# Attention and expert layer on one core: the maxima are transposed in the value bank, and the latents' softmax is normalised behind its product with the values

## What is computed

```python
local  = softmax over the last 128 keys (q k / 4) @ v          # 16 heads
pooled = mean of every 16 tokens                               # 64 latents a batch
lscores = rq rk / 4, only latents of earlier chunks allowed    # 4 heads of 16
lattn  = softmax(lscores);  lattn = 0 where no latent is allowed
remote = (lattn @ rv) @ rout_w + rout_b
gate   = sigmoid(local @ gl_w + remote @ gr_w)
mixed  = gate * local + (1 - gate) * remote
x1     = x + ga * (mixed @ out_w + out_b)
```

## Time and profile before

| what | value |
|---|---|
| median of the runs shown | 576.77 us (572.23 to 577.25, 3 runs) |
| the profiled execution's own time | 576.64 us |
| its span, first to last instruction | 574.9 us |
| busy: PE, DVE, ACT, POOL | 84%, 76%, 62%, 66% of the span |
| mean granted TensorE clock | 0.949 of full speed |

### The profile page before, as it was taken

How to read it: one execution, slowest core, us unless ns; L and a number is a source line. 1 busy time by engine, 2 the same in 40 slices (tenths; PEclk the granted TensorE clock), 3 DMA queues, 4 the chain that set the end, 5 groups by cost and what they waited for, 6 DMA issues and landing times.

```text
span 574.9 us, 19855 instructions
## 1 busy us (share of the span) xinstructions
PE 482.9 (84%) x7168; PEld 364.1 (63%) x7168; DVE 436.6 (76%) x1193; ACT 353.8 (62%) x868; POOL 379.2 (66%) x516
## 2 busy tenths in 40 slices
PE   2446689999899999999999999999999999988771
PEld 2205567777677666777777676777776676766451
DVE  2155657788688888988988788888888887878554
ACT  1210466677677667777777577777776776766540
POOL 2222346778577767788877587777777677766663
PEclk9975889999899999999999899999999999999776
DMA  9558644618244444434252607162534444440000
GB/s 277 114 133 246 163 105 99 132 47 187 56 113 75 95 94 93 94 90 93 64 101 68 119 34 145 39 125 62 120 68 97 92 94 93 82 79 10 11 10 19
DMA packets 56523, 55.15 MB, mean 96 GB/s; under 512 B 7380, under 2 KB 53100, under 8 KB 54892
## 3 DMA queue, kind: packets, MB, share of 16 engines
q1 hardware_dynamic: 53564, 52.57, 41.4%
q10 hardware_dynamic: 2864, 1.31, 1.1%
HBM read 37.07 MB, written 16.80 MB: 94 GB/s over the span
## 4 chain that ended last, share of the span: by engine, by line
PE 72%; issue 11%; POOL 5%; DVE 4%; DMA 2%; ACT 2%; ACTq 1%; SPq 1%; POOLq 0%; DVEq 0%
PE p_pv L819 9%; PE p_qkv L730 9%; PE p_qkv L740 6%; PE p_misc L886 6%; PE p_y L806 5%; PE p_x L785 5%; PE p_y L807 5%; PE p_x L778 4%; PE p_a L751 3%; PE p_qkv L860 3%; PE p_misc L869 2%; PE p_a L831 2%; PE p_a L716 2%; PE p_misc L877 2%; PE p_a L753 2%
## 5 line engine op out<-in xcount | busy, mean ns | idle before, releaser
L592 ACT ACTIVATE pr<-p_y 128x512 f32<-128x512 f32 x224 | 124.6, 595 | 55.8 <-PE p_y L807 52.9
L1159 DVE TENSOR_REDUCE mtok<-p_x 128x3 bf16<-128x480 f32 (+1 forms) x192 | 109.3, 585 | 30.9 <-PE p_x L785 29.6
L441 POOL TENSOR_SCALAR_AFFINE_SELECT pr<-pr 128x512 f32<-128x512 f32 x128 | 89.6, 701 | 11.2 <-ACT pr L594 9.0
L451 POOL TENSOR_TENSOR rstd<-ve,half 128x1 f32<-128x1 f32 x96 | 58.1, 605 | 47.9 <-DVE ve L1079 47.7
L469 POOL TENSOR_TENSOR dif<-local,rem 128x272 f32<-128x272 f32 x32 | 30.9, 965 | 83.8 <-DVE local L1197 83.8
L445 POOL TENSOR_SCALAR_AFFINE_SELECT pr<-pr 128x512 f32<-128x512 f32 x112 | 81.3, 726 | 0.0
L807 PE MATMUL p_y<-qst,kst 112*128 112x128 bf16 x512 | 73.2, 221 | 0.0
L806 PE MATMUL p_y<-qst,kst 112*128 112x128 bf16 x448 | 66.5, 221 | 7.7 <-ACT pr L592 4.8
L819 PE MATMUL p_pv<-pr,vp 128*18 128x128 f32 x1920 | 67.1, 279 | 2.1 <-POOL pr L445 0.8
L730 PE MATMUL p_qkv<-hT,wqk 128*128 128x256 f32 x256 | 66.1, 403 | 2.2 <-DVE qkf L1111 1.3
L740 PE MATMUL p_qkv<-wv,hT 128*128 128x272 f32 x128 | 40.1, 439 | 29.5 <-issue 29.4
(11 more groups left out here) (131 smaller groups left out, 1092.7 us busy)
## 6 DMA issues: line engine op xcount, KB each, us to landing
scr_q<-terms SPq DMA_DIRECT2D x16, 384.0 KB, 2.5
qst<-scr_q SPq DMA_DIRECT2D x16, 384.0 KB, 4.7
scr_k<-terms SPq DMA_DIRECT2D x16, 384.0 KB, 4.4
kst<-scr_k SPq DMA_DIRECT2D x16, 384.0 KB, 5.4
qst<-scr_q SPq DMA_DIRECT2D x16, 256.0 KB, 5.4
kst<-scr_k SPq DMA_DIRECT2D x16, 256.0 KB, 6.4
out_y<-y SPq DMA_DIRECT2D x32, 128.0 KB, 1.7
x_all<-in_x SPq DMA_DIRECT2D x3, 1024.0 KB, 8.3
```

The costliest lines, as they stand in the source:

```text
L441: ins = pool.affine_select(out=own, in_=own, compare_op=ALU.is_ge, fill=0.0, base=-1, pattern=[[0, 4], [1, P]], channel_multiplier=-1)
L592: act.activation(pr[:, 2 * i:2 * i + 2, :, :], src, ACT.Exp).then_inc(exp_done[i], 1)
L1159: dve.tensor_reduce(mtok[:, KS + h0:KS + h1], p_x[i % 2][:, 0:(h1 - h0) * w].rearrange("p (h n) -> p h n", n=w), AX_X, ALU.max, negate=Tru ...
```

## The change

- `max_t` writes to `p_pv` instead of `p_qkv`, and stands behind part 1 of the scores instead of ahead of it. It waits for `oT_ready` of the tile before (`out_t` has emptied the bank). `mtok` has two buffers now. `shift` reads `p_pv`; ScalarE's list keeps its order but for what is removed.
- `project_v` waits for `rem_ready` of k-3 instead of `shift`; `lat_remote` waits for `shift` no more.
- The latents' softmax is not divided before its product with the values. `lat_exp` sums no rows, `lat_p_t` transposes the exponentials `le` themselves, and `bvd` has 64 more columns of ones by head, so that `lat_out_t` puts the sums of each head into rows 64 to 127 of `p_misc`. `lat_recip` is now the reciprocal of these 64 x 128 values, `lat_norm` the product with it, and both work on tile `m` on VectorE between `norm1` and `maxima` part 3. The product writes `loT`; ScalarE's `lat_oT` is gone. In the first tile of a batch 16 columns are set to zero by an instruction of their own.
- In the setup four copies put the ones into the two buffers of `bvd` and of a new `bvd1` (for tiles that see 32 latents).

```diff
@@ ScalarE
-                act.activation(q_of(t)[KS:KS + H, :, :], p_qkv[KS:KS + H, 0:P // 2]...
+                act.activation(q_of(t)[KS:KS + H, :, :], p_pv[KS:KS + H, 0:P // 2]...
...
-                act.wait_ge(lp_ready, done(t - 1))
+                act.wait_ge(lpT_psum, done(t - 1))
                 for h in range(LH):
-                    ins = act.activation(..., ACT.Exp, bias=lneg[:, h:h + 1], accum_out=lsum[:, h:h + 1])
+                    ins = act.activation(..., ACT.Exp, bias=lneg[:, h:h + 1])
...
-            def lat_oT(t):
-                act.wait_ge(loT_psum, done(t))
-                act.wait_ge(rem_psum, done(t - 1))
-                act.activation(loT[0:LD, :], p_misc[0:LD, 0:P], ACT.Copy).then_inc(loT_ready, 1)
@@ TensorE
             def project_v(t):
-                pe.wait_ge(shift_ready, done(t - 2))
+                pe.wait_ge(rem_ready, done(t - 3))
...
             def max_t(t):
                 pe.wait_ge(s_max[LAST_MAX], done(t))
-                pe.wait_ge(qk_copied, done(t + 3))
-                pe.wait_ge(rem_ready, done(t - 1))
-                pe.transpose(p_qkv[:, 0:P // 2].bitcast(BF16), mtok[:, :], ident_bf[:, :]).then_inc(mT_psum, 1)
+                pe.wait_ge(oT_ready, done(t - 1))
+                pe.transpose(p_pv[:, 0:P // 2].bitcast(BF16), mtok[:, t % 2, :], ident_bf[:, :]).then_inc(mT_psum, 1)
...
             def lat_p_t(t):
-                pe.wait_ge(lp_ready, done(t))
+                pe.wait_ge(lexp_ready, done(t))
...
             def lat_remote(t):
                 pe.wait_ge(loT_ready, done(t))
-                pe.wait_ge(shift_ready, done(t))
...
             def slot(t, stages):
+                if S:
+                    scores(t, 1)
                 if T:
                     max_t(m)
                 if S:
-                    scores(t, 1)
                     scores(t, 0)
                     lat_scores(t)
@@ VectorE
+                      *[dve.tensor_copy(bvd[:, r, :, LD:2 * LD], ...) for r in range(2)],
+                      *[dve.tensor_copy(bvd1[:, r, LD:2 * LD], ...) for r in range(2)],
...
             def lat_recip(t):
-                dve.wait_ge(lexp_ready, done(t))
...
-                    dve.reciprocal(lrec[:, :], lsum[:, :]).then_inc(lval_ready, 1)
+                dve.wait_ge(loT_psum, done(t))
+                dve.reciprocal(rden[:, :], p_misc[LD:2 * LD, 0:P]).then_inc(rden_ready, 1)
...
             def lat_norm(t):
-                dve.tensor_tensor(by_head(lp, t), by_head(le, t), bc(lrec[:, :], seen(t)), ALU.mult).then_inc(lp_ready, 1)
+                dve.wait_ge(rden_ready, done(t))
+                dve.wait_ge(rem_psum, done(t - 1))
+                if t % NB:
+                    dve.tensor_tensor(loT[0:LD, :], p_misc[0:LD, 0:P], rden[:, :], ALU.mult).then_inc(loT_ready, 1)
+                else:
+                    dve.tensor_scalar(loT[0:LD, 0:CH], rden[:, 0:CH], 0.0, None, ALU.mult)
+                    dve.tensor_tensor(loT[0:LD, CH:P], p_misc[0:LD, CH:P], rden[:, CH:P], ALU.mult).then_inc(loT_ready, 1)
```

More of the change, by code:

```diff
@@ L50 @@
 SU_SILU, SU_MODT, SU_ROWS = 3, 9, 22
-SU_PRE = SU_ROWS + 13
+SU_PRE = SU_ROWS + 17
 SU_ALL = SU_PRE + B // 2
@@ L62 @@
 C_IND = C_RV1 + LD
-C_VAL = C_IND + P
-C_BRK = C_VAL + 1
+C_BRK = C_IND + P
 C_BD = C_BRK + 1
@@ L139, in build @@
         bvd = sb("bvd", [P, 2, 2, P])
-        mtok = sb("mtok", [P, P], BF16)
+        bvd1 = sb("bvd1", [P, 2, P])
+        mtok = sb("mtok", [P, 2, P], BF16)
         pr = sb("pr", [P, H, 2, P])
@@ L144, in build @@
         le = sb("le", [P, LH * LT])
[L145 to L148 removed]
+        rden = sb("rden", [LD, P])
         lpT = sb("lpT", [P, 2 * P])
@@ L221, in build @@
         ls_psum, lmx_ready, lexp_ready = counted("ls_psum", "PE"), counted("lmx_ready", "DVE"), counted("lexp_ready", "ACT")
-        lval_ready, lp_ready = counted("lval_ready", "DVE"), counted("lp_ready", "DVE")
-        lrec_ready = sem("lrec_ready")
+        rden_ready = counted("rden_ready", "DVE")
         lpT_psum, lpT_ready = counted("lpT_psum", "PE"), counted("lpT_ready", "ACT")
-        loT_psum, loT_ready = counted("loT_psum", "PE"), counted("loT_ready", "ACT")
+        loT_psum, loT_ready = counted("loT_psum", "PE"), counted("loT_ready", "DVE")
         rem_psum, rem_ready = counted("rem_psum", "PE"), counted("rem_ready", "ACT")
@@ L262, in seen, with values_of @@
             return LT // 2 if t % NB < NB // 2 else LT
+        def values_of(t):
+            return bvd[:, t % 2, :, :] if seen(t) == LT else bvd1[:, t % 2:t % 2 + 1, :]
         def by_head(ap, t):
@@ L650, in slot @@
                     shift(m)
-                    lat_oT(m)
                 if S:
@@ L1023, in weights @@
                       dve.memset(loT[LD:LD + 1, :], 1.0),
+                      *[dve.tensor_copy(bvd[:, r, :, LD:2 * LD], cst[:, C_RV:C_RV + 2 * LD].rearrange("p (k l) -> p k l", k=2))
+                        for r in range(2)],
+                      *[dve.tensor_copy(bvd1[:, r, LD:2 * LD], cst[:, C_RV1:C_RV1 + LD]) for r in range(2)],
                       dve.tensor_copy(rqT[LD:P, 0, :], cst[LD:P, C_IND:C_IND + P]),
@@ L1270, in slot @@
                     norm1(a)
+                if T:
+                    lat_recip(m)
+                    lat_norm(m)
                 if S:
@@ L1293, in slot @@
                     shift2(d)
-                if S:
-                    lat_norm(t)
                 if D:
```

29 lines of the change are left out of this document (8 added, 21 removed).

## The result

The kernel after takes 594.25 us (median of four runs, 592.81 to 596.25), the one before on the same chip 576.35 (four runs, 572.23 to 577.25): a ratio of 1.0346 [1.0296, 1.0396]. That is slower by 3.5%; the two medians alone are 17.9 us apart, which is 3.1%. The forecast was 589.5 within 583 to 602, and within 576 to 602 in 8 cases of 10. The profiled span is 593.7 us, 18.8 more than before.

The account below looks back on a forecast made before the run. It took a ring through `local_out`, `difference` and POOL's masks to set the slot. Slots with 64 latents 7.8, with 32 2.6, batch starts 0.9, last slots 1.0, setup 0.55: 12.9 on 576.64 gives 589.5 us, range 583 to 602.

Parts of the forecast that it names:

- What bounds the kernel: Whole slot: a change is worth what it does to the start of `local_out`, counted from the slot's start; slot 15.41 us.
- the ring: 15.41 us slot: `sum_v`, `out_t`, `part2`, `shift`, `project_v`, `out_tokens`, `local_out`, `difference`, masks, `sum_v`; TensorE not setting its end.
- The transposition's wait: TensorE: `max_t` stands for `out_t` until about +0.78, making `lat_scores` 0.48 us later; `project_v` loses its 0.83 us wait.
- `lat_max` to the end of `norm1`: VectorE, slot with 64 latents: 1.65 us from `lat_max` at +2.07 to the end of `norm1` at +3.72.
- The reciprocal: VectorE, ahead of `local_out`: new 64 x 128 reciprocal taken as 1.0 us, possibly 0.28 to 1.25.
- Product to `local_out`: VectorE and TensorE: product gives `loT` at +5.04, `prob_sum` at +5.90, `local_out` at +6.40 instead of +5.60, 0.80 us later.
- What comes back on POOL: POOL's masks: 0.15 us a slot shorter with the division of `lp` gone; could be nothing, up to 0.36.
- The third rival: Masks: another part of the ring gives most of the delay back, 585 or 580 us; chance of second step 0.10.
- The second rival: VectorE: the reciprocal runs at the product's rate, 0.28 us, so 574 us, within 1% of before; chance 0.12.
- the first: Rival on TensorE: the removed `project_v` wait pays, 547 us in full or 560 within TensorE's slack; chance 0.05.
- The sum: Whole program: 7.8 + 2.6 + 0.9 + 1.0 + 0.55 = 12.9 us more, giving 589.5 us, 2.2% slower.
- the 0.65 for a slot with 64 latents: Delay per slot in 12 slots with 64 latents and the full chain: 12 x 0.65 = 7.8 us.

Follow-up runs that it names:

- the run of 557.22: Value-bank part only on the kernel before, transposition behind `lat_scores`, SP's queries' loads ahead of the store of y in even slots: 557.22 us, 0.9655.
- the table: Slot 13 of the kernels before, after, each part alone, copy for the reciprocal, and three with the transposition late: slots of 14.64 to 16.36 us.
- the bank alone: Kernel before plus only the value-bank part (maxima transposed there, `project_v` not waiting for `shift`), latents as before: 574.34 us, 0.9945.
- latents alone: The change with the maxima's transposition put back in its old bank and place, against the kernel before: 581.37 us, 1.0111.
- before with the earlier terms: Kernel before with only ScalarE's `part2` moved ahead of `out_t` and POOL's `part3` ahead of `rstd1`: 571.37 us, 0.9934.

## Why the prediction was right, and which terms were mis-sized

**What bounds the kernel.** Right in the count, wrong in the engine. The slot is the start of `local_out` plus 9.7 to 9.8 us, as I had it, and both costs of the change, the wait for `out_t` and the reciprocal ahead of `out_tokens`, came as forecast. But I closed the ring over `difference` and POOL's masks, and I set TensorE aside because the weight loads of `sum_v` wait 10.3 us for the last masks. That row is no slack of TensorE: it is there in the same size in the run of 557.22, where TensorE is never idle in slot 13.

```profile
PEld p_pv L816 <- POOL pr L443: 10.4, 27, 0.8
```

In slot 13 the loads stand 0.33 us there in every kernel of the table, though the last mask has ended 0.15 to 0.21 us earlier; the matmuls of `sum_v` themselves wait only 0.8 us for L445 in the whole kernel before. TensorE's own list makes the slot from `out_tokens` on. That my sum served even so is luck: `local_out` and `out_tokens` move together, so a count from either gives the same shift.

**The transposition's wait.** Right in kind: L787 stands behind `oT`, `project_v` waits no more. I put its start at +0.78; it is +0.88, since 0.15 us pass from the end of `out_t` to it. `lat_max` is at +2.17 where I said +2.07.

**`lat_max` to the end of `norm1`.** Mis-sized, and the largest miss in a slot. I took 1.65 us, by the start of the maxima that follow `norm1`; but VectorE starts those 0.08 us ahead of `norm1`'s end, and it starts the reciprocal 0.03 behind it. And `norm1` itself grew, from 0.82 us in slot 15 before to 0.93:

```profile
286.59 0.82 DVE L1094 TENSOR_SCALAR xn<-x_all,mv,rstd 128x256 f32<-128x256 f32 x1
```

In the rows of slot 13 after it begins while POOL's `ux` runs, and ends at 266.83, 0.15 us behind the end of `xb` (266.68); before, it ended 0.15 behind `ux`. From `lat_max` to the reciprocal it is 1.86 us. I moved an instruction and kept its duration.

**The reciprocal.** 0.96 for 1.0 us: right, by the rows of narrower ones. From 16 to 128 columns the trace gives (959 - 253) / 112 = 6.3 ns a column. The Trainium skill, "Vector Engine (DVE) Microarchitecture Reference", section 5.2, would have it at an estimated 0.21 us; the measurement decides against that for this operation. "VectorE: DVE Perf Modes", section "First, the fixed hardware budget", which calls it an iterative divide, agrees with the trace as far as it goes: the copy of the same size takes 293 ns.

**Product to `local_out`.** Right: the product ends at +5.31 for my +5.04, `prob_sum` is at +6.15 for +5.90, `local_out` at +6.62 for +6.40. From the reciprocal on the shift of about 0.25 us is only handed through.

**What comes back on POOL.** Too much, and for a wrong reason: I took 0.15 us a slot off the masks; from `difference` to the last mask it is 0.03 in the mean of the twelve full slots, and less work on POOL does not shorten these slots. From the start of `local_out` to the slot's end it is 0.06 us less than before in the eleven without slot 6, only because `local_out` starts 1.22 us behind `out_tokens` instead of 1.14. The third rival, which lived on the masks, is out: the mask that was left out altogether gave nothing back in a full slot. The second rival falls with the 959 ns, the first with the wait at L787.

**The sum.** Between the two profiled executions, from the slots' lengths: eleven full slots gave 0.99 each, 10.9 us (I had 0.65 for each of twelve); the twelfth, slot 6, gave -1.15. The four slots 3, 11, 19, 27 gave 1.8, slots 10, 18, 26 gave 2.3. The six that start a batch or follow one gave 1.2, for 0.9. The last slots gave 0.3 for 1.0; the start of slot 2 came 0.57 us earlier, where I had put 0.55 for the setup. That makes 14.8 of the 18.8, for my 12.9; the rest is slot 2 with +4.1, which I had not seen. So 589.5 came as near as it did by errors of both signs. In slots 6 and 17 (-0.98) the kernel before had delays of its own that the change doesn't show: its trace has a granted clock of 0.50 for 3.4 us in each (147.3 to 150.7 and 318.0 to 321.4), behind a stand of TensorE of 2.58 us in slot 6, and in slot 17 behind one of 1.26 us that slots 9 and 25 have too. What made the stand of slot 6, and the fall in slot 17, was not tried.

So the term that was off is the 0.65 for a slot with 64 latents, which measured 0.99. Of the 0.34 between, 0.10 is the handover from `out_t` to the transposition, 0.21 the stretch from `lat_max` to the reciprocal, -0.04 the reciprocal, 0.09 what I took off the masks and did not get, and the rest rounding and the way to `local_out`.

**Slot 2.** The keys' stack is late: the store of its terms is issued at 72.70 us, at 70.95 before. TensorE, order of time:

```profile
83.58 0.27 PE L771 MATMUL p_x<-edge,ident_bf 128*32 128x192 bf16 x4 [2.11 <-issue]
```

And the windows around it:

```profile
72.00:83.50 11.50, 7.67 (x126) 5.54 (x125) 6.07 (x17) 7.43 (x20) 5.66 (x8) 1.00 0.57 105
84.30:91.10 6.80, 6.80 (x68) 4.94 (x60) 4.76 (x11) 3.79 (x7) 0.27 (x1) 0.50 0.18 60
```

Behind the stand the granted clock is 0.50, its level of 1.2 GHz, for 6.8 us; before, that stretch was granted 1.00, and 0.50 only ahead of slot 2, from 72.2 to 75.6, so the earlier start of slot 2 is not the price of the setup alone. The stand belongs to the part on the value bank: all the traces with that part have it (1.17 to 2.38 us; 1.55 with the bank alone), and the three without it don't (before, latents alone, before with the earlier terms). Why the terms of slot 1 come 1.75 us later with it stays open: VectorE's copy out of the projection for them waits longer for TensorE, and I have followed it no further.

## What to carry to other kernels

In a ring that runs over several engines, find the one start to which a slot's length is tied, and price an edit by what it does to that start. Then see which engine has no idle time from there to the slot's end: work taken off another engine, as the mask here, gives nothing back in such slots. Price both parts of an edit together, since each may hide in room that the other takes. An instruction put into an in-order queue ahead of its data delays all that is behind it: the same 0.22 us transposition held nothing up two steps later. When the ring is freed, look at once for what was hidden behind it: here a transfer queue, whose order had to change before slots of 14.99 and 14.64 us made the program 1.5 and 3.5% shorter than the kernel before.
